# Last attention units and FFN: rows normalised on GpSimd, alternating adders, scaling in quarters

## The reference

```python
x = x + attn(layernorm(x), w_qkv, w_out, b_out)     # 1 x 2048 x 128, 16 heads of 64
x = x + ffn(layernorm(x), w_gate, w_up, w_down)     # width 352

def fp4_quant_dequant(x):                           # blocks of 16 along the last dim
    scale = max(max(abs(block)) / 6, 1e-12)
    idx = searchsorted(MID, abs(block / scale))
    return GRID[idx] * sign(block / scale) * scale  # GRID 0 .5 1 1.5 2 3 4 6
def fp4_linear(x, w):
    return fp4_quant_dequant(x) @ fp4_quant_dequant(w).T
h = silu(fp4_linear(x, w_gate)) * fp4_linear(x, w_up)
ffn = fp4_linear(h, w_down)
```

## Time and profile before

| | us |
|---|---|
| three runs, median (lowest, highest) | 1327.34 (1326.15, 1327.88) |
| the profiled execution | 1330.24 |
| its span | 1328.4 |
| a regular unit, such as 27 | 36.75 |
| start of the last unit / its end | 1210.5 / 1241.7 |
| sums' matmuls end, normalised output there | 1246.4 / 1250.5 |
| exp of one tile (L685), mean | 1.03 |
| last exps (13; 14 and 15) begin | 1235.98; 1238.43 |
| two reciprocals (L879) between two maxima, unit 29 | 1.77 |
| reciprocals of the last sums, four, and L887 behind them | 3.39, 0.69 |

### The profile page before, as it was taken

The page is one execution under the profiler, slowest core; times in us unless marked ns, Lnnn a source line. Parts: engine busy times, 40 slices in busy tenths (PEclk is TensorE's granted clock), DMA queues, the critical chain, the costliest instruction groups (busy, mean ns, idle before and its releaser), DMA issues.

```text
span 1328.4 us, 24703 instructions
## 1 busy us (share of the span) xinstructions
PE 1256.3 (95%) x7405; PEld 664.9 (50%) x7405; DVE 910.3 (69%) x2386; ACT 882.3 (66%) x1244; POOL 1036.6 (78%) x464
## 2 busy tenths in 40 slices
PE   4999999999999999999999999999999999798676
PEld 3555555555455555555455555555545544444335
DVE  6766767677666666667666666666766667778788
ACT  5767676677666767667667767677767667564443
POOL 4488888988888888888788888898888887876333
PEclk9999999999999999999999999999999999999888
DMA  2000000000000000000000000000000000000001
GB/s 64 2 10 1 1 2 10 1 1 2 3 10 1 1 2 10 1 2 2 3 10 1 1 2 10 1 2 2 1 3 1 1 2 1 1 1 1 0 1 33
DMA packets 45953, 6.68 MB, mean 5 GB/s; under 512 B 37344, under 2 KB 45664, under 8 KB 45808
## 3 DMA queue, kind: packets, MB, share of 16 engines
q1 hardware_dynamic: 45584, 4.41, 2.6%
q0 software_dynamic: 224, 0.54, 0.1%
HBM read 3.75 MB, written 1.05 MB: 4 GB/s over the span
## 4 chain that ended last, share of the span: by engine, by line
PE 84%; DVE 8%; issue 6%; ACT 1%; POOL 1%; DMA 0%; POOLq 0%; SPq 0%; DVEq 0%; ACTq 0%
PE o_ps L1273 32%; PE s_ps L1114 25%; PE mx_ps L1136 8%; PE mx_ps L1129 4%; PE misc_ps L1263 3%; PE misc_ps L1251 2%; PE misc_ps L1101 2%; PE misc_ps L1079 2%; PE s_ps L1122 1%; PE misc_ps L1081 1%; PE misc_ps L1080 1%; PE s_ps L1360 1%; DVE scaled L801 1%; DVE split L798 1%; DVE amax L823 1%
## 5 line engine op out<-in xcount | busy, mean ns | idle before, releaser
L567 POOL TENSOR_TENSOR acc_pool<-acc_pool,probs 128x1024 f32<-128x1024 f32 x343 | 829.6, 2419 | 50.7 <-POOL acc_pool L567 40.4
L685 ACT ACTIVATE probs<-s_ps 128x1024 f32<-128x1024 f32 x512 | 524.9, 1026 | 67.2 <-PE s_ps L1114 44.0
L862 DVE CUSTOM_DVE_ANT_0 summed<-mx_ps,rise 128x512 bf16<-128x512 f32 x503 | 344.6, 685 | 281.4 <-issue 237.4
L1273 PE MATMUL o_ps<-probs,vv 128*64 128x512 f32 x2048 | 495.5, 604 | 0.1
L605 ACT ACTIVATE rise<-mx_ps 128x512 f32<-128x512 f32 x503 | 300.1, 597 | 277.5 <-PE mx_ps L1129 269.5
L1273 PEld LDWEIGHTS o_ps<-probs,vv 128*64 128x64 f32 x2048 | 127.2, 136 | 222.5 <-issue 182.6
L1136 PE MATMUL mx_ps<-k_hi,q_hi 64*128 64x512 f32 x503 | 223.4, 444 | 14.0 <-issue 9.3
L1129 PE MATMUL mx_ps<-k_raw,q_hi 64*128 64x512 f32 x503 | 224.3, 446 | 7.4 <-DVE part_max L862 7.4
L1114 PE MATMUL s_ps<-q_hi,k_hi 64*128 64x512 f32 x1024 | 207.3, 396 | 0.0
L1114 PE MATMUL s_ps<-q_hi,k_lo 64*128 64x512 f32 x1024 | 205.8, 393 | 0.0
L1114 PE MATMUL s_ps<-q_lo,k_hi 64*128 64x512 f32 x1024 | 205.1, 392 | 0.0
(11 more groups left out here) (176 smaller groups left out, 1102.7 us busy)
## 6 DMA issues: line engine op xcount, KB each, us to landing
mrow<-neg_max SPq DMA_DIRECT2D x256, 0.5 KB, 2.0
wqkv<-in_L_attn_w_qkv SPq DMA_DIRECT2D x8, 192.0 KB, 2.9
y<-in_L_attn_x SPq DMA_DIRECT2D x4, 256.0 KB, 4.2
out<-y SPq DMA_DIRECT2D x4, 256.0 KB, 2.6
wo<-in_L_attn_w_out SPq DMA_DIRECT2D x8, 64.0 KB, 1.9
wx<-in_L_ffn_w_down POOLq DMA_DIRECT2D x1, 176.0 KB, 5.9
wx<-in_L_ffn_w_gate POOLq DMA_DIRECT2D x1, 128.0 KB, 4.7
wx<-in_L_ffn_w_up POOLq DMA_DIRECT2D x1, 128.0 KB, 5.7
```

Source lines behind the costliest of these rows:

```text
L567: pool.tensor_tensor(acc, first, probs[:, j % P_BUFS, :, :], ALU.add) \
L685: act.activation(probs[:, j % P_BUFS, :, :], s_ps[:, j % 2, :, :], ACT.Exp, scale=SCALE) \
L862: dve.tensor_tensor_reduce(summed[:, s % 2, :], mx_bank(h, pair), rise[:, h, :], 1.0, LOWEST, ALU.add, ALU.max, part_max[:, slot:slot + 1] ...
L1273: ins = pe.matmul(o_ps[DH * h:DH * (h + 1), :], vv[par(w)][:, j, DH * h:DH * (h + 1)], probs[:, j % P_BUFS, h, :], start=(j == 0), stop=(j ...
```

## The change

It touches the last turn from w = 4 on, and the FFN.

1. **Adders.** In w = 5 and 6 GpSimd adds ten tiles in place of twelve, VectorE six in place of four, and they alternate (`LAST_POOL`). w = 4 and 7 keep their tiles.
2. **Sums stay apart** from w = 4 on (`separate`): no combining addition on GpSimd, two more matmuls in `misc("den")`. GpSimd's additions there are made in halves of 512 columns.
3. **Rows on GpSimd.** In w = 5 to 7 the four row tiles are normalised by GpSimd behind the roots; VectorE waits for them at j = 12 ahead of the block scales. GpSimd's `over_scale` moves from j = 10 to 11 (12 in w = 7), `times_scale` from 2 to 4; ScalarE's sign and size from j = 13 to 14; grid steps shift by one.
4. **Quarters.** For h, `over_scale` and `times_scale` go in four instructions of 352 columns; `ht` waits for its own quarter. For the last h, size and grid go in two halves.
5. **Orders.** TensorE: both first transposes ahead of the last `den`; T3 earlier. ScalarE: a Silu on a small tile behind the last output copy, which brings the table load there. VectorE: the last x group's grid ahead of the inversion, `hidden` 0 and 1 ahead of the projection's addition, 2 to 5 between the parts of the last normalisation.

```diff
+LAST_POOL = {4: list(range(POOL_TILES - 1)), 5: [0, 1, 2, 4, 5, 7, 8, 10, 11, 13], 6: [0, 1, 2, 4, 5, 7, 8, 10, 11, 13],
+             7: list(range(0, STEPS - 2, 2))}
-PE_ORDER = ([("T", 0), ("T", 1), ("gu", 0), ("gu", 1), ("proj", 0), ("T", 2)] + [("gu", k) for k in range(2, 12)]
+PE_ORDER = ([("T", 0), ("T", 1), ("den", 0), ("gu", 0), ("gu", 1), ("proj", 0), ("T", 2)] + [("gu", k) for k in range(2, 10)]
+            + [("T", 3)] + [("gu", k) for k in range(10, 14)] + [("ht", 0), ("gu", 14), ("ht", 1), ("down", 0), ("gu", 15)]
...
-ACT_ORDER = ([("T", 0), ("T", 1), ("silu", 0), ("silu", 1), ("T", 2), ("sign", 4), ("abs", 4)]
...
+ACT_ORDER = ([("T", 0), ("T", 1), ("silu", 0), ("silu", 1), ("T", 2), ("silu", 2), ("silu", 3), ("silu", 4), ("sign", 4), ("abs", 4)]
+             + [("silu", 5), ("sign", 5), ("silu", 6), ("abs", 5), ("silu", 7), ("silu", 8), ("silu", 9), ("T", 3)]
+             + [("sign", 6), ("silu", 10), ("silu", 11), ("abs", 6), ("silu", 12), ("silu", 13), ("ht", 0), ("sign", 7), ("silu", 14)]
+             + [("ht", 1), ("silu", 15), ("abs", 7), ("ht", 2), ("sign", 8), ("ht", 3), ("ht", 4), ("ht", 5), ("abs", 8)]
+             + [("ht", 6), ("ht", 7), ("abs", 9)] + [("ht", k) for k in range(8, 16)])
...
+        def separate(w, last):
+
+            return last and w >= CHUNKS
...
+        def pieces(n):
+
+            return TQ if QUANTS[n][0] == "h" else 1
...
+                for i in range(TQ):
+                    n = g * TQ + i
+                    ins = pool.tensor_scalar(fx[:, i * DIM:(i + 1) * DIM], y[:, n, :], mv[:, n, 0:1], root[:, 1, n:n + 1],
+                                             ALU.subtract, ALU.mult)
+                ins.then_inc(rows_ready, 1)
...
+                        if separate(w, last):
+                            pool.tensor_tensor(acc[:, 0, :], first[:, 0, :], probs[:, j % P_BUFS, 0, :], ALU.add)
+                            pool.tensor_tensor(acc[:, 1, :], first[:, 1, :], probs[:, j % P_BUFS, 1, :], ALU.add) \
+                                .then_inc(pool_adds, 1)
...
-                        if last and w >= FIRST_ROWS and j == 2:
+                        if last and w >= FIRST_ROWS and j == 4:
                             times_scale(w - FIRST_ROWS)
                         if last and w >= FIRST_ROWS and j == 8:
                             roots(w - FIRST_ROWS)
-                        if last and w >= FIRST_ROWS and j == 10:
+                        if last and w >= FIRST_ROWS and j == (12 if w == BODY - 1 else 11):
                             over_scale(w - CHUNKS)
...
-                        if last and (w, j) == (CHUNKS, 7) or last and w >= FIRST_ROWS and j == 13:
+                        if last and (w, j) == (CHUNKS, 8) or last and w >= FIRST_ROWS and j == 14:
                             signs(w - CHUNKS)
                             sizes(w - CHUNKS)
...
+            act.activation(warm[:, 1:2], warm[:, 0:1], ACT.Silu)
...
-                            if j == 10:
-                                dve.wait_ge(root_ready, g + 1)
-                                normalised(tiles, fx)
-                            if j == 11:
+                            if j == 12:
+                                dve.wait_ge(rows_ready, g + 1)
                                 block_scales(g + 1)
...
+            hidden(0)
+            hidden(1)
             add_projection(ITERS - 1, BODY, True)
             dve.wait_ge(misc_free, misc_no(ITERS - 1, BODY, "proj", True) + START + 1)
-            quant_x(GROUPS - 1)
...
+            moments(ends)
+            hidden(2)
+            inverse_root(ends)
+            hidden(3)
+            normalised(ends, fx)
+            block_scales(QUANTS.index(("x", GROUPS - 1)))
+
+            hidden(4)
+            block_scales(QUANTS.index(("h", 0)))
+            hidden(5)
```

More of the change, by code:

```diff
@@ L336, in pool_tiles, with dve_tiles @@
         def pool_tiles(w, last):
-            return POOL_TILES - 1 if last and CHUNKS <= w < BODY - 1 else POOL_TILES
+            return LAST_POOL.get(w, list(range(POOL_TILES))) if last else list(range(POOL_TILES))
+        def dve_tiles(w, last):
+            return [t for t in range(STEPS) if t not in pool_tiles(w, last)]
         def extra(w, last):
-            return max(w - CHUNKS, 0) if last else 0
+            return sum(POOL_TILES - len(pool_tiles(v, last)) for v in range(w))
         def pool_at(it, w, last, plus=0):
@@ L404, in before, with quants @@
             return max((m for m in range(n) if buf(m) == buf(n)), default=None)
+        def pieces(n):
+            return TQ if QUANTS[n][0] == "h" else 1
+        def quants(n):
+            return sum(pieces(m) for m in range(n))
         def part_of(n, part):
@@ L557, in body @@
                     acc = acc_pool[:, w % 2, :, :]
-                    end = last and w == BODY - 1
-                    for k, j in enumerate(END_POOL[1:] if end else range(1, pool_tiles(w, last))):
-                        if k == 0:
+                    for k, j in enumerate(pool_tiles(w, last)[1:]):
+                        if k == 0 and not separate(w - 1, last):
                             pool.wait_ge(den_acc, after(it, 1, w, 1))
@@ L1323, in _, with transpose_x @@
             body(ITERS - 1, True)
-            misc("den", ITERS - 1, BODY, True)
+            def transpose_x(n):
+                pe.wait_ge(f_quant, quants(QUANTS.index(("x", n)) + 1))
+                if n:
+                    pe.wait_ge(f_xt_copied, n)
+                else:
+                    pe.wait_ge(mx_free, max_no(ITERS - 1, BODY - 2, MAX_STEPS - AHEAD) + 1)
+                for t in range(TQ):
+                    row = (n * TQ + t) * DIM
+                    ins = pe.transpose(banks[4][:, t * P:(t + 1) * P], xq[:, row:row + DIM], ident[:, :])
+                ins.then_inc(f_xt, 1)
             def transpose_h(k, g):
@@ L1345, in _ @@
                 if what == "T":
[L1347 to L1353 removed]
+                    transpose_x(n)
+                elif what == "den":
+                    misc("den", ITERS - 1, BODY, True)
                 elif what == "gu":
```

179 lines of the change are left out of this document (85 added, 94 removed).

## The result

The changed kernel takes 1322.95 us (median of 10 runs, 1321.0 to 1325.9), the kernel before 1327.34; the ratio is 0.9966, with a 95% interval from 0.9957 to 0.9976. So it is faster, but by 4.4 us where 15.5 were forecast.

A forecast was written before the change was run, and what follows sets the result against it. TensorE, 95% busy, bounds the regular units; at stake were the last units and the FFN, held by VectorE. Terms -2.5 - 3.2 - 3.8 + 2.9 - 7.8 - 1.1 = -15.5 off the 1327.3 median: 1312 us, range 1301 to 1324.

The forecast's parts named there:

- (a): GpSimd's additions in halves: 1.25 us each, 0.1 to 0.3 dearer per tile, some 2 us of GpSimd in a unit.
- (e): Rows on GpSimd, units 29 to 31: 0.4 us each, 1.7 for four; some 3 us margin, so exp doesn't wait.
- rival 2: Units 28 to 30 and FFN: every wait is a full one, GpSimd always coming back first; 1323.5 us, chance 20%.
- Unit 28, -2.5: Unit 28 (w = 4, last turn): 2.5 us back of the 5 over its own work; bounds 0 and 4.
- the lock: GpSimd and VectorE exclude each other: a VectorE instruction reading SBUF data waits for the whole GpSimd instruction, up to 2.4 us.
- Unit 29, -3.2: Unit 29 (w = 5): stall and slow clock gone -8.0, products +0.9, overshoot +3.9; net -3.2 us, bounds -6 and +1.
- (c): Working for unit 29: VectorE's five additions overshoot ahead of the next maximum, 3.9 us net new; unit -3.2 us.
- Unit 30, -3.8: Unit 30: as unit 29 without Q, overshoot at tiles 12 and 15 free; -3.8 us, bounds -6 and +1.
- rival 3: Units 29 to 31: GpSimd rows are dear, slower from 1.7 us each, 1335 us at 2.3; chance 7%.
- (f) and (g), +2.9: Unit 31 and entry: exp 15 ends 3.9 us late, sums wait behind transposes and table load; y's addition +2.9 us.
- FFN, -7.8: FFN from y's addition to last grid value: orders -5.2 and -1.0, quarters -2.0, waiting products +0.4; -7.8 us.
- Rival 1: Units 29 to 31, entry and FFN: waits are short and exp 15 isn't held; 1303 us, chance 15%.

The follow-up runs named there:

- rows_dve: Changed kernel with the row tiles of units 29 to 31 normalised on VectorE again, GpSimd only making the roots: 1315.60 us.
- rows_twice: Changed kernel with each GpSimd row instruction of units 29 to 31 made twice, the second into a buffer nothing reads: 1332.75 us.
- ffn_only: Changed kernel with attention put back as in the kernel before, keeping only the changed FFN and end: 1318.35 us.
- combo_rows_dve: Changed kernel with whole additions, tile 3 on GpSimd, sign and size behind exp 15, sums before transposes, rows on VectorE: 1307.73 us.

## Why the prediction was wrong, point by point

The forecast's sign held, and so did the FFN's part; the size was three and a half times too large. What failed is the attention part: units 28 to 31 and the entry were to give 6.6 us and cost 5.0 more. The steps that were wrong are the price of GpSimd's work, in (a) for halves and in (e) for rows, and the conclusion of (e) that GpSimd keeps a margin of 3 us, so that exp doesn't wait. That 1322.95 lies in the range at all is luck, as the point on rival 2 below says. My sum against the spans: -15.5 forecast, -4.9 measured.

- **Unit 28, -2.5: wrong, +0.9.** The step that failed is (a): 0.1 to 0.3 for a tile in halves, 2 us in a unit. It was 0.38 and 4.5: the pieces' own 0.18 lay in my bounds, but I let only VectorE wait at the lock there and left out that GpSimd waits for VectorE as well. exp then waited 7.5 us. With whole additions the unit gains 1.1, so the other 1.4 of my 2.5 wasn't there either.
- **Unit 29, -3.2: -2.9 in the profiled pair, -1.8 by the means, and from other terms.** The stall of 9.99 went, as told; in its place came exp 7 waiting 2.3 for VectorE's paired addition, and the size step 3.8 for GpSimd. The wait of exp stood nowhere in my working. Its sum has a slip as well: the overshoots that (c) lists, 2.0, 1.9, 0.5 and 0.8, make 5.2 and not 5.7, so by them the unit would be at -3.8. The clock was 0.98.
- **Unit 30, -3.8: wrong, -0.1 in the profiled pair, -1.7 by the means.** The same two waits (2.6 and 3.5), and exp's 2.5 for GpSimd. With rows on VectorE it is 38.56, with tile 3 moved 38.99: either alone gives about what I had forecast, 38.5.
- **(e), rows at 0.4: wrong by two.** They cost 0.79 each. I chose by the share of columns in an addition; two scalars for each partition aren't an addition. My upper bound, 1.03, held. "28 us of work in units of 39" became 33, and with that fell "so exp doesn't wait". My rival 3 had the right place and kind of cost and a threshold of 1.7 us for each, which took GpSimd's time as free up to there. `rows_dve` and `rows_twice` show that it isn't free: taking 3 us off each unit or adding 3 moved the time by 7.4 and 9.8.
- **(f) and (g), +2.9: wrong in size, +7.1.** The chain was as told (rows, tiles 10 and 12, product, size, exp 15), and from the first row to the product's end it took 11.7 us, where I had added up 11.6, but of other terms: the rows 3.74 and not 1.7, the waits for VectorE 1.8 and not 3.6. Exp 15 ended 6.0 later than before, counted from the unit's start, and not 3.9, because the chain began late. I took the roots from the old timeline, as if all ahead of them stayed; they ended 22.7 us into the unit, where they had ended at 20.7 before (I had read 20.4). Exp 8 begins 1.4 later in the unit as well, and y's addition 2.2; no run separates what of that is the second pair of products for unit 30's sums. To that comes the clock, which I hadn't priced. Behind the 4.9 us with TensorE busy for 0.15 the granted clock was 0.50, and the last four products with the values took 1.98 us, where the four before them took 1.08, and the sums 1.98 + 1.54, where `ffn_only` has 1.08 + 1.03. The kernel before had some of it too: a clock of 0.71 from 1241.7 to 1250.0, and 1.08 + 1.62 for its sums. The table load's place was right.
- **FFN, -7.8: better, -9.8.** The orders gave 7.2 (6.2 forecast), the quarters 2.6 (2.0). A split step of 1408 columns took 1.16 (I had said 1.2 to 1.6).
- **The end, -1.1: -0.6.** Quarter 14's transpose starts earlier, as said; the stores behind it are as before.
- **Ahead of unit 28** the profiled execution of after is 0.5 later, in code that is the same.

The misses: 3.4 + 3.7 + 4.2 for units 28, 30, and 31 with the entry, 0.5 at the end, 0.5 at the start, 0.3 in unit 29, less 2.0 in the FFN: 10.6, which is the whole of 15.5 - 4.9. Rival 2, every wait a full one, gives the right time (1323.5) for the wrong reason: the FFN, where it wanted +4, did better than forecast, and unit 31 with the entry, where it wanted no more than my sum, was 4.2 worse. That they cancel is luck. Rival 1, that exp 15 isn't held, is out: it was held for 3.8 us.

The Trainium skill (GPSIMD Engine Reference, section 8, Key points) calls VectorE about twice as fast for elementwise work. The additions agree (2.42 and 1.21 for 1024 columns); the rows don't (four in 3.13, against 1.1 in the earlier trace rows, nearly three times). By its figure they would have been 2.2 us for four and not 3.1: the page pointed the right way, and less far than it was. The same skill (SBUF — State Buffer, "SBUF: two separate sides") has the lock held by whoever starts first while the other blocks fully. That is symmetrical, and the halves of 2.14 and 2.24 beside VectorE's additions agree; I had read it from VectorE's side alone.

What stays open: of the change's parts, the alternating adders and the sums kept apart were never run by themselves, so what they are worth is not shown, and neither is GpSimd's product ahead of tile 12's addition in unit 31, where it stood before. Unit 31 is still 1.5 us longer in `combo_rows_dve` than before, of which the second pair of products for unit 30's sums would make 0.8 to 1.0, an estimate by the earlier trace rows. And since units 29 and 30 differ by up to 1.6 us between executions of the same code, the gain of a single edit there is known to about that.
